# Another hand-written order for the first eleven steps of a four-layer graph network, and two more waits on VectorE

## What is computed

```
# layer 0: attention
h = relu(layernorm(x)); Wh = h @ W; e = leaky_relu(Wh @ a1 + (Wh @ a2).T)
att = softmax(where(adj > 0.5, e, -9e15), axis=1);  x = x + elu(att @ Wh)
# layer 1: normalised graph convolution
h = relu(layernorm(x)); Ah = adj + I; d = rsqrt(sum(Ah))
x = x + relu(d * Ah * d.T @ h @ K1 + bias)
# layer 2
h = relu(layernorm(x)); x = x + relu(adj @ h @ K2) * (row of h is not all zero)
# layer 3: mean over the neighbours
h = relu(layernorm(x)); x = x + relu(concat(h, adj @ h / sum(adj)) @ W3.T)
```

## Time and profile before

| | |
|---|---|
| median of three runs | 2527.27 us |
| the profiled execution | 2537.66 us, span 2535.9 us, 1.8 us around it |
| PE (TensorE) busy | 2483.5 us, 98% |
| DVE (VectorE) busy | 2049.3 us, 81% |
| ACT (ScalarE) busy | 1401.9 us, 55% |
| POOL (GpSimd) busy | 1238.8 us, 49% |
| PE not busy | 52.4 us |
| chain that ended last, by engine | PE 38%, DVE 21%, SPq 17%, DMA 13% |

### The profile page before, as it was taken

How to read it: one execution, slowest core, us unless ns; L and a number is a source line. 1 busy time by engine, 2 the same in 40 slices (tenths; PEclk the granted TensorE clock), 3 DMA queues, 4 the chain that set the end, 5 groups by cost and what they waited for, 6 DMA issues and landing times.

```text
span 2535.9 us, 40566 instructions
## 1 busy us (share of the span) xinstructions
PE 2483.5 (98%) x13106; PEld 2135.4 (84%) x13106; DVE 2049.3 (81%) x4371; ACT 1401.9 (55%) x2571; POOL 1238.8 (49%) x1608
## 2 busy tenths in 40 slices
PE   5999999999999999999999999999999999999999
PEld 4888888888888888888888888888888888888887
DVE  8988887887887888888888888888878788887863
ACT  5655555555555555555555555555555555555543
POOL 4655444554554445545545544445455455445441
PEclk9999999999999999999999999999999999999999
DMA  3222222212222122222222222222222222222200
GB/s 125 67 51 61 60 55 60 61 51 67 52 60 67 50 59 61 57 60 61 55 63 53 59 67 49 62 58 56 62 61 55 63 57 55 67 52 60 55 21 30
DMA packets 350978, 148.63 MB, mean 59 GB/s; under 512 B 274864, under 2 KB 315184, under 8 KB 350768
## 3 DMA queue, kind: packets, MB, share of 16 engines
q1 hardware_dynamic: 350768, 146.03, 23.0%
HBM read 80.87 MB, written 33.61 MB: 45 GB/s over the span
## 4 chain that ended last, share of the span: by engine, by line
PE 38%; DVE 21%; SPq 17%; DMA 13%; issue 5%; POOL 5%; ACT 0%; POOLq 0%; DVEq 0%
PE O L379 18%; SPq L310 15%; PE T L379 14%; DMA wh_dram<-wh 7%; DMA wh_rows<-wh_dram 6%; PE X L379 6%; DVE ln_stats L841 5%; POOL xs L1161 3%; DVE p_lo L897 3%; DVE act_out L934 2%; DVE t_lo L903 2%; DVE act_out L911 2%; SPq L315 1%; DVE scores L876 1%; DVE xs L937 1%
## 5 line engine op out<-in xcount | busy, mean ns | idle before, releaser
L1191 POOL TENSOR_TENSOR h_lo<-h,h_hi 128x512 fp32r<-128x512 f32 x384 | 553.2, 1461 | 382.9 <-ACT h_hi L582 382.7
L576 ACT ACTIVATE h<-xs,ln_bias,ln_scale 128x512 f32<-128x512 f32 x512 | 395.8, 811 | 425.4 <-POOL ln_bias L1184 425.3
L379 PE MATMUL O<-w_hi,t_hi 128*128 128x512 f32 x1536 | 600.3, 391 | 6.5 <-DVE t_lo L903 6.4
L379 PE MATMUL O<-w_hi,t_lo 128*128 128x512 f32 x1536 | 599.3, 390 | 0.0
L379 PE MATMUL O<-w_lo,t_hi 128*128 128x512 f32 x1536 | 599.1, 390 | 0.0
L588 ACT CAST t_hi<-T 128x512 fp32r<-128x512 f32 x512 | 298.3, 583 | 388.0 <-PE T L379 388.0
L903 DVE TENSOR_TENSOR t_lo<-T,t_hi 128x512 fp32r<-128x512 f32 x512 | 345.6, 685 | 194.1 <-ACT t_hi L588 192.4
L1155 POOL TENSOR_TENSOR xs<-xs,act_out 128x512 f32<-128x512 f32 x128 | 165.5, 1313 | 537.0 <-ACT act_out L616 519.8
L841 DVE BATCH_NORM_STATS2 ln_stats<-xs 128x6 f32<-128x512 f32 x512 | 332.1, 681 | 30.6 <-POOL xs L1161 28.4
L379 PEld LDWEIGHTS O<-w_hi,t_hi 128*128 128x128 f32 x1536 | 289.3, 188 | 62.9 <-issue 7.5
L379 PEld LDWEIGHTS O<-w_hi,t_lo 128*128 128x128 f32 x1536 | 289.2, 188 | 60.4
(11 more groups left out here) (105 smaller groups left out, 5056.4 us busy)
## 6 DMA issues: line engine op xcount, KB each, us to landing
xs<-x SPq DMA_DIRECT2D x64, 512.0 KB, 5.3
out<-xs SPq DMA_DIRECT2D x63, 512.0 KB, 4.1
h<-act_out SPq DMA_DIRECT2D x960, 32.0 KB, 1.9
a_raw<-adj_t SPq DMA_DIRECT2D x64, 256.0 KB, 2.7
a_rows<-adj SPq DMA_DIRECT2D x64, 256.0 KB, 2.7
wh_rows<-wh_dram SPq DMA_DIRECT2D x59, 128.0 KB, 4.4
z<-w_all SPq DMA_DIRECT2D x3, 512.0 KB, 4.1
xs<-w_all SPq DMA_DIRECT2D x3, 512.0 KB, 10.2
```

The costliest lines, as they stand in the source:

```text
L379: last = nc.tensor.matmul(psum, s, m, start=(start and n == 0 and i == 0), stop=(stop and n == len(pairs) - 1 and i == 2))
L576: nc.scalar.activation(h[:, k.odd, m], xs[:, k.xb, m], ACT.Relu, bias=ln_bias[:, k.quad, m:m + 1], scale=ln_scale[:, k.quad, m:m + 1], acc ...
L1191: nc.gpsimd.tensor_tensor(h_lo[:, k.odd, m], h[:, k.odd, m], h_hi[:, k.odd, m].bitcast(F32), ALU.subtract).then_inc(h_lo_ready, 1)
```

## The change

The calls of the fill are put in another order on TensorE, ScalarE, VectorE and GpSimd. No call is added or taken away. SyncE's queue, the loop and the drain stay. Two waits come in on VectorE, in the fill and in the loop: `mask_scores` waits until the low parts of the attention ahead are made (it overwrites `scores`, from which they are read), and `with_self` until both `a_lo` of the step of layer 1 ahead are made. Both are for work of VectorE's own queue.

```diff
--- before.py
+++ after.py
@@ -500,22 +500,22 @@
     spread(step(0))
     spread(step(1))
     gather(step(0))
+    spread(step(2))
     project(step(0))
     gather(step(1))
-    spread(step(2))
     project(step(1))
     gather(step(2))
     project(step(2))
     gather(step(3))
+    project(step(3))
+    gather(step(4))
     spread(step(5))
-    gather(step(4))
-    project(step(3))
+    project(step(4))
     gather(step(5))
-    project(step(4))
     project(step(5))
     gather(step(6))
+    gather(step(7))
     project(step(6))
-    gather(step(7))
     project(step(7))
     gather(step(8))
     transpose_h(step(9))
@@ -663,61 +663,61 @@
 
     split_weight(0)
     activate(step(0))
+    split_weight(1)
+    high_part(step(0))
     activate(step(1))
-    split_weight(1)
     exps(step(0))
-    high_part(step(0))
+    activate(step(2))
+    split_weight(2)
     high_part(step(1))
+    exps(step(1))
     both(step(0))
-    exps(step(1))
-    activate(step(2))
+    split_weight(3)
+    elu_half(step(0), 0)
     high_part(step(2))
-    elu_half(step(0), 0)
     elu_half(step(0), 1)
     both(step(1))
-    split_weight(2)
     exps(step(2))
     elu_half(step(1), 0)
+    with_self(step(3))
     elu_half(step(1), 1)
-    split_weight(3)
-    with_self(step(3))
     both(step(2))
     activate(step(3))
     high_part(step(3))
+    split_weight(4)
+    elu_half(step(2), 0)
     activate(step(4))
+    with_self(step(4))
+    both(step(3))
+    elu_half(step(2), 1)
+    with_self(step(7))
     high_part(step(4))
-    with_self(step(4))
-    split_weight(4)
+    without_self(step(6))
     activate(step(5))
-    elu_half(step(2), 0)
-    both(step(3))
+    both(step(4))
     high_part(step(5))
-    elu_half(step(2), 1)
-    without_self(step(6))
     exps(step(5))
+    activate(step(6))
     split_weight(5)
-    both(step(4))
-    without_self(step(8))
-    with_self(step(7))
+    high_part(step(6))
     both(step(5))
+    activate(step(7))
+    with_self(step(11))
     split_weight(6)
-    activate(step(6))
-    high_part(step(6))
-    split_weight(7)
-    activate(step(7))
     high_part(step(7))
     elu_half(step(5), 0)
+    without_self(step(8))
+    split_weight(7)
     both(step(6))
+    split_weight(8)
     elu_half(step(5), 1)
     activate(step(8))
...
@@ -866,6 +866,7 @@
 
     def mask_scores(k):
         dve.wait_ge(mask_ready, k.done(L0))
+        wait(dve, p_lo_ready, k.done(L0, NT, back=1))
         if k.g < SPREAD:
             wait(dve, wh_rows_ready, k.done(L0))
             row = blocks(wh_psum)
@@ -972,6 +973,7 @@
         raw_diag, raw_rest = flat_blocks(a_raw[:, k.ab])
         wait(dve, a_loaded[k.ab], 16 * (k.g // A_BUFS + 1))
         wait(dve, ah_hi_ready, k.done(L1, 2, back=1))
+        wait(dve, ah_lo_ready, k.done(L1, 2, back=1))
         nc.vector.tensor_tensor(a_diag[:], raw_diag, ident[:].unsqueeze(1).to_broadcast([P, NT, P]),
                                 ALU.add).then_inc(diag_ready, 1)
         wait(dve, ah_hi_ready, k.part(L1, 2, 0))
@@ -995,69 +997,69 @@
     vector_columns(0)
     vector_columns(1)
     statistics(step(0))
+    add_mask(step(0))
     vector_rows()
     statistics(step(1))
     dots(step(0))
-    add_mask(step(0))
+    statistics(step(2))
     mask_scores(step(0))
+    add_mask(step(1))
     dots(step(1))
     softmax_parts(step(0))
-    add_mask(step(1))
-    statistics(step(2))
+    mask_scores(step(1))
     degrees(step(0))
-    mask_scores(step(1))
+    dots(step(2))
     both(step(0))
+    split_weight(2)
     add_mask(step(2))
-    degrees(step(1))
+    split_weight(3)
     softmax_parts(step(1))
-    dots(step(2))
+    mask_scores(step(2))
     positive_part(step(0))
     both(step(1))
-    mask_scores(step(2))
     statistics(step(3))
     softmax_parts(step(2))
+    degrees(step(1))
+    with_self(step(3))
     positive_part(step(1))
+    both(step(2))
+    statistics(step(4))
+    statistics(step(5))
     degrees(step(2))
-    with_self(step(3))
-    statistics(step(4))
-    both(step(2))
-    statistics(step(5))
+    split_weight(4)
     add_mask(step(5))
-    split_weight(2)
     with_self(step(4))
-    split_weight(3)
+    both(step(3))
+    with_self(step(7))
+    positive_part(step(2))
     dots(step(5))
-    both(step(3))
+    scaled_relu(step(3))
     mask_scores(step(5))
-    positive_part(step(2))
-    split_weight(4)
-    softmax_parts(step(5))
     both(step(4))
-    with_self(step(7))
-    scaled_relu(step(3))
     statistics(step(6))
     statistics(step(7))
+    softmax_parts(step(5))
+    scaled_relu(step(4))
     both(step(5))
-    scaled_relu(step(4))
-    statistics(step(8))
+    degrees(step(5))
+    with_self(step(11))
     without_self(step(6))
     split_weight(5)
-    degrees(step(5))
+    statistics(step(8))
     both(step(6))
+    split_weight(6)
+    without_self(step(8))
...
@@ -1203,38 +1205,38 @@
 
     normalise(step(0))
     normalise(step(1))
-    low_part(step(0))
     split_weight(1)
     normalise(step(2))
+    low_part(step(0))
+    low_part(step(1))
     degrees(step(0))
-    low_part(step(1))
+    elu(step(0))
     low_part(step(2))
-    elu(step(0))
     normalise(step(3))
     elu(step(1))
     degrees(step(1))
+    low_part(step(3))
+    normalise(step(4))
+    normalise(step(5))
     degrees(step(2))
-    normalise(step(4))
-    low_part(step(3))
-    normalise(step(5))
     low_part(step(4))
+    elu(step(2))
     low_part(step(5))
-    elu(step(2))
     normalise(step(6))
     normalise(step(7))
     low_part(step(6))
+    degrees(step(5))
+    low_part(step(7))
+    mask_rows(step(6))
     normalise(step(8))
-    mask_rows(step(6))
-    low_part(step(7))
     elu(step(5))
...
```

More of the change, by code:

```diff
@@ L686, in _ @@
             high_part(step(3))
+            split_weight(4)
+            elu_half(step(2), 0)
             activate(step(4))
+            with_self(step(4))
+            both(step(3))
+            elu_half(step(2), 1)
+            with_self(step(7))
             high_part(step(4))
-            with_self(step(4))
-            split_weight(4)
+            without_self(step(6))
             activate(step(5))
-            elu_half(step(2), 0)
-            both(step(3))
+            both(step(4))
             high_part(step(5))
-            elu_half(step(2), 1)
-            without_self(step(6))
             exps(step(5))
+            activate(step(6))
             split_weight(5)
-            both(step(4))
-            without_self(step(8))
-            with_self(step(7))
+            high_part(step(6))
             both(step(5))
+            activate(step(7))
+            with_self(step(11))
             split_weight(6)
-            activate(step(6))
-            high_part(step(6))
-            split_weight(7)
-            activate(step(7))
             high_part(step(7))
             elu_half(step(5), 0)
+            without_self(step(8))
+            split_weight(7)
             both(step(6))
+            split_weight(8)
             elu_half(step(5), 1)
             activate(step(8))
-            with_self(step(11))
             high_part(step(8))
+            both(step(7))
             masked_relu(step(6))
-            both(step(7))
             activate(step(9))
@@ L719, in _ @@
             transposed(step(9))
-            split_weight(8)
             activate(step(10))
@@ L1046, in _ @@
             both(step(6))
+            split_weight(6)
+            without_self(step(8))
+            split_weight(7)
             positive_part(step(5))
-            without_self(step(8))
-            with_self(step(11))
-            split_weight(6)
-            split_weight(7)
             both(step(7))
@@ L1054, in _ @@
             statistics(step(10))
+            split_weight(8)
             add_mask(step(10))
-            statistics(step(11))
             both(step(8))
@@ L1059, in _ @@
             dots(step(10))
-            split_weight(8)
+            statistics(step(11))
             for j in slots[FILL - FIRST:]:
@@ L1232, in _ @@
             normalise(step(9))
-            degrees(step(5))
+            mask_rows(step(8))
             normalise(step(10))
+            low_part(step(10))
             normalise(step(11))
-            mask_rows(step(8))
-            low_part(step(10))
             for j in slots[FILL - FIRST:]:
```

## The result

| | us |
|---|---|
| changed kernel, median of 10 | 2531.77 (2529.66 to 2537.21) |
| kernel before, median of 10 on the same chip | 2525.39 (2523.86 to 2528.82) |
| ratio | 1.0026, 95% interval 1.0018 to 1.0034 |
| the profiled execution of the changed kernel | 2532.58, span 2530.8 |
| forecast, range | 2529.0, 2521.5 to 2533.0 |

The changed kernel is 6.4 us slower, 0.26%, a little more than the 0.2% at which I had put a difference that can be told. The time lies in the range, but slower by more than 0.2% was a result to which I gave 0.13. The profiled execution of before, 2537.66, was 12 us above the median of its kernel measured now. Sums must be held against stretches that both kernels share, not against the spans.

What follows compares the result with a forecast made beforehand. TensorE paces the loop, so the fill decides. Running sum against before: +0.7 at P0, -6.1 at P2's end, +3.3 at P5's end, +2.4 at G8, +1.8 at G10; 2527.27 + 1.8 = 2529.1, stated as 2529.0, range 2521.5 to 2533.0.

Steps and rivals of the forecast that it cites:

- The mark: Start of G10, first still-waiting gather with the same queue place in both kernels: 129.77 us before, 131.6 forecast, +1.8.
- the loop's waits: The two added VectorE waits in the loop: taken as met or hidden in VectorE's idle time, 0 us.
- the bound of 5.7: Upper cost of a loop wait: 0.1 us of lost overlap each, all 57 on the path, +5.7 us.
- the late half 8: Rival, chance 0.12 with other late loop-entrance work: late load of weight half 8 delays P7, +5.6 us, 2532.9.
- P5: Product in the fill: starts at 91.9, ends at 97.4 against about 94.1 before, +3.3, 9.4 given back.
- G8 to G10: End of the fill: half 8's cast and difference leave the chain, statistics of step 11 enter; 14.0 us against 14.5.
- Up to P2: Start of the fill: +0.7 at P0, P2's stall 3.6 to 0.4, slow clock gone; P2 ends at 60.4, -6.1.
- P3: Product after G3: waits 2.1 us for ScalarE's split, held behind step 4's activate; starts 65.4, ends 71.0.
- P4: Product after G4: step 5's dots held by four GpSimd instructions; stall 6.3 us, start 80.2, slow clock, 8.2 long.
- P5 to G8: Three gathers and two products: 20.2 us from P5's end to G8's end against 21.1 before, leaving +2.4.
- The front gain: Rival, chance 0.22: dots of step 5 miss GpSimd's instructions, P4's stall 2.6, clock stays up; -4.6, 2522.7.
- It does nothing because VectorE is the bound: Rival, chance 0.14: stalls in the fill are only renamed and the terms cancel, 0; 2527.3.

Runs made afterwards that it cites:

- e1: Kernel before plus both added VectorE waits, nothing moved: 2536.12 us, ratio 1.0016 against the kernel before.
- h1: Changed kernel's order up to the split of step 2 and P2, the kernel before's order behind it, both waits: 2537.37 us, ratio 1.0007 against before.
- e6: Kernel before plus the two added waits in the loop only: 2525.50 us, ratio 1.0002 against before.
- e5: Changed kernel with step 3's split ahead of step 4's activate and adjacency on ScalarE, and ahead of that adjacency on VectorE: 2537.54 us, ratio 1.0020 against before.
- e4: Changed kernel with GpSimd's update of graph 2 moved behind the low part of step 5: 2539.34 us, ratio 1.0014 against before.
- e2: Changed kernel with statistics of step 11 ahead of step 8's split, and its normalisation ahead of low_part(10): 2534.81 us, ratio 1.0014 against before.
- h2: Kernel before's order up to the split of step 2 and P2, changed kernel's order behind it, both waits: 2546.06 us, ratio 1.0043 against before.
- e3: Changed kernel with step 4's VectorE split directly behind the dots of step 5: 2537.18 us, ratio 1.0023 against before.
- e9: Changed kernel with e2, e3 and e5 together, scores ahead of relu, softmax ahead of statistics of steps 6 and 7: 2528.92 us, ratio 1.0016 against before.
- e8: Changed kernel with the two added waits in the fill only: 2530.10 us, ratio 1.0016 against before.
- e10: Repeat of e1, the kernel before plus both added waits: 2538.24 us, ratio 1.0010 against before.
- e7: Kernel before plus the two added waits in the fill only (steps up to 11): 2524.59 us, ratio 1.0001 against before.

## Why the prediction was right, and where it was not

**The mark, and the loop.** Right: the loop is TensorE's, and what is lost ahead of it reaches the end. But the mark was set one block too early. The sum took G10 to be equally long in both kernels; it ran at a PEclk of 0.61 now and of 1.00 before, which adds 1.3 us to the 5.3 (less 0.1 for the start) and gives the 6.4 of the end. In all six kernels with a wait of 2.74 to 2.83 ahead of G10 it lasted 4.1 to 4.4 us; behind 2.36 to 2.39 it took 3.2 in four kernels and 4.4 in e1 and h1. The term for the loop's waits, 0, held, as e6 shows (1.0002), though the bound of 5.7 counted 57 of them and there are 119.

**Luck.** The sum said +1.8 and the kernel lost 6.4. The time is inside the range only since its upper edge, 2533.0, came from a rival, the late half 8, which didn't happen. What filled that room was two mis-sized terms, P5 later by 1.8 and the stretch from G8 to G10 longer by 1.7, and G10's 1.3, for which the sum had no term.

**Up to P2.** Right in kind: P2 starts with no wait at a PEclk of 1.00, G3 5.3 us earlier (I had 6.1). Of the 0.8, 0.7 was lost ahead of P0. I priced the scores of graph 1 at 1.1 beside GpSimd's low part, but both small instructions of theirs were held:

```profile
30.07 1.24 DVE L881 SCALAR_TENSOR_TENSOR s_neg_max<-s_max,wh 128x2 f32<-128x2 f32 x1
31.34 1.20 DVE L884 SCALAR_TENSOR_TENSOR s_neg<-s_neg_max 128x2 f32<-128x2 f32 x1
```

In before the first of the two took 0.16 us and the second 1.11, and I had not counted the first as work that can wait.

**P3.** Wait 3.11, not 2.1. The low part of step 3 ended at 61.3 instead of 60.2, and the power in step 4's normalisation took 1.64 us beside VectorE's split of a weight, where it takes 0.71 alone. GpSimd is held as well as VectorE; I had priced one side only. I also left the clock at full behind this wait, and it fell (0.54). With the wait gone, in e5, P4 gains only 0.8 of the 3.9, and the end is not told apart from that of the changed kernel (1.0020 against 1.0026, in two sessions).

**P4.** Right, and it is the step on which the forecast stood: the first dot 0.85 us and then three held for 1.77 each, a long wait ahead of P4 and the low clock behind it. The wait is 4.68 and not 6.3 only because P3 was late and slow, so that G4 ended later. P4 is 2.2 us later than forecast, as P3 is 2.0 later: the dots of step 5 start at 70.73 where I had 69.1, since their `activate` stood behind the casts that P3 waited for. e4 takes away just the two holds whose partners it moves, 2.2 us. With two holds instead of all of them, which is as many as the rows of before show, the sum would have been that much smaller. The Trainium skill ("SBUF — State Buffer", SBUF: two separate sides) says that the pair of ports is an exclusive lock, which goes for the whole instruction to whichever starts first, an instruction of VectorE with two inputs in SBUF or one of GpSimd that reads SBUF. The trace agrees three times in a row here, 1.77 us against 0.68.

**P5 to G8.** From P5 to the end of G8, 25.7 us forecast and 25.7 measured (93.75 to 119.4). Half 8 was not late: ScalarE's cast of it ran at 102.8 without a wait.

**G8 to G10.** This is the term that was mis-sized: 14.0 forecast, 15.7 measured, 14.5 before. I counted the statistics of step 11 as 1.6 us on VectorE, and did not ask who waits for them. GpSimd normalises from them, and ScalarE's `activate(11)`, which waits for that and is first in the loop's queue, holds the exponentials of step 10. e2 takes it away: the exponentials' 1.8 us come back, and the whole stretch takes 13.1 instead of 15.7. The 1.7 us of this term and the 1.8 by which P5 was late are the 3.5 us by which G10 was missed.

**The rivals.** The front gain did not stay. Half 8 was no cause. "It does nothing because VectorE is the bound" is refuted, by the 6.4 us and by h2, which has the same work and loses 10.3: VectorE was busy 107.8 us of 14 to 129.7 us before, and now 101.0 of 14 to 135.1, since it came to stand itself. Its waits ahead of G10 (total, times, longest), now:

```profile
DVE t_lo L904 <- ACT t_hi L588: 7.1, 8, 2.6
DVE ln_stats L841 <- POOL xs L1163: 3.0, 2, 2.1
DVE a_lo L980 <- ACT a_hi L650: 2.7, 2, 2.4
```

My reading, which no run tests as a whole, is that in a list that was full before, the moved pieces had been each other's cover. The two waits that I took as 0 cost 0 to 4 us, not settled; no median reached the bound of 5.7 that I kept for them. As to the chances: the mean of my cases lay at about no change. A second piece of work that had gone behind something late, as at G10, is likelier than I gave it in a list with a hundred moved calls; slower by over 0.2% deserved more than 0.13.

## What to carry to other kernels

When an order is written out by hand for several queues, a stall taken away at one block tends to stand again at the next (P2 to S5 in h1, P4 to G5 in e3, to P5 in e9); compare the start of a late common mark, not the stall that was mended, and put the mark behind the last block that can run at another clock (here G11, not G10). Of every call that is moved back, ask who consumes its result and what stands behind that consumer on its own queue: the two mistakes here, the statistics of step 11 and in e9 those of step 6, were both a small instruction for which ScalarE held back something urgent. And where VectorE and GpSimd both read SBUF, count holds on either side, for small instructions as for large ones.

## What the runs showed of the hardware

- A 128x2 instruction of VectorE takes 0.16 us, or 1.24 to 1.27 when GpSimd's low part has started ahead of it; who is first was decided by 0.03 us.
- GpSimd is held too: its power of 128x2 took 1.64 us instead of 0.71, its two-instruction low part 2.99 to 3.38 beside the dots and 2.5 without them.
- The clock after a wait is not the same in each execution. In the changed fill P0 follows waits of 1.4 to 1.9 us ahead of S2 and 0.26 ahead of itself, and lasted 7.15 us in after, e3 and h1, 5.55 in e2, e4, e5, e8 and e9. The two groups differ ahead of the wait. In the first the last three or four matmuls of G0 already took 0.28 us each instead of 0.41, that is the clock had risen before the wait of 1.84 to 1.92, and in P0 it was down again (0.54). In the second all of G0 ran slow, S2 waited 1.42 to 1.44, and P0 had the full clock. (The level in G0 is read from its matmuls: the PEclk of its windows says 1.00 throughout, in before too, where it lasted 5.5 us for 24 matmuls that take 2.9 at G5.)
- P2 behind a wait of 3.61 to 3.70 us lasted 8.2 us in before, 8.3 in e10, 7.2 in e6 and e7, and 5.5, at the full clock, in e1. A wait of 2.09 was enough for 1.2 GHz in part of e4's P4. A price for a drop is a chance, and in this fill it is worth 1.3 to 2.7 us.
- The kernel before had medians of 2524.8 to 2535.7 us in different sessions, most of it in the time behind G10. A change of 0.2% in it can only be seen beside the kernel before on the same chip at the same time.
